# An attention stack on one core: phases written out, additions waited for one by one, values projected straight into the form in which they are used

## The chip, the core and the metric

One core of a Trainium2 chip. The kernel is one program; its time is the device time in microseconds (us) from start to end of the program. The engines are called as in the profile: PE (TensorE matmul), PEld (its weight load), DVE (VectorE), ACT (ScalarE), POOL (GpSimd) and SP (SyncE, which here only issues DMAs; SPq in the rows).

## The reference

The input is x, of 4 batches by 256 channels by 1024 positions, float32. Four attention layers follow one another. Layers 0 and 1 have one head each. Layers 2 and 3, which the change concerns, have eight heads of 32 channels:

```python
xn = group_norm(x) * gn_w + gn_b            # 32 groups
q, k, v = split(qkv_w @ xn + qkv_b)         # per head: 32 channels each
weight = softmax((q * s).T @ (k * s))       # 1024 x 1024 per head
a = weight @ v
hout = proj_w @ a + proj_b
return xn + hout                            # layer 2; layer 3 is x + hout in the same form
```

Each softmax row sums to one, so a constant added to every value (the value bias) comes through the attention unchanged.

## The kernel before

Layers 2 and 3 are done in one section (`eight_heads_in`). The work comes in 16 groups: 2 layers, 4 batches, 2 groups of 4 heads. A batch of a layer (two groups) is a round here. Each group has a phase of 64 steps. In one step PE makes one score tile (128 keys by 512 queries of one head, L1054), and ACT takes its exponential into a ring of four key tiles `PR` (L1226). A phase has two halves of the queries of 32 steps; in each half the eight key tiles (four heads each) pass through the ring. A key tile takes four steps.

For each key tile PE weighs the values (`weigh`, L957): four matmuls by 32 columns, one for each head, side by side in the array, into `psO`. In the profile a float32 matmul stands as two records, so a tile is 8 records and two tiles together 16. The sums of the exponentials are made in two ways. POOL adds key tiles 0 to 5 of a half in five additions into `PA` (L1268); the sum over keys of `PA` and of the last two tiles is made on PE by a matmul with ones (`sums`, L969, 24 records), which is the side unit "z". DVE then turns and inverts it and scales `psO` (`take_half`).

Beside the scores, PE does side units, each at a step of a table (`SIDE_AT`, `Z_AT`, `BN_AT`, `XN_AT`), in order, through four banks of `psD`:

- "m" and "a": 64 of them in a phase, score tiles of a later group (L1023), of which DVE takes the maxima (L1105). `EARLY` says how many of them stand in the phase before.
- "K", "Q": projections of the next group, 6 matmuls in each half (L89), taken by ACT into `SL` (L1191). ACT splits them into a high part `SH` (L1178), POOL makes the low part (`low`, L1251), and SP copies both by 24 DMAs into `KS` and `QS` (`stack`, L1298 and L1300). The next "K" must wait until these copies have landed (`stacks_filled`).
- "v", "w": in each phase the values of one group. "v" projects a half with channels on partitions (6 matmuls of 512 columns), ACT adds the bias into `VT`; "w" turns it round by four PE transposes (L1017), and ACT copies it into `V`.
- "p" in every second phase: the output projection of the round before (4 units). "t", "T": turned maxima.

In every second phase the next batch is normalised as well: POOL makes the factors, ACT writes the input at the steps of `XN_AT`, POOL makes its low part `XL` (L1245). Where layer 2 ends, POOL also splits the weights of layer 3 (L1277), which PE's next "K" waits for.

The waits around the change: before the first exponential of a key tile ACT waits for what is still read in its slot of the ring. At the first four tiles of a phase it waits for all five additions of the phase before:

```python
wait(e, av_done, weighed(P, J - 4))
if J >= 4: ...
else:
    wait(e, sum_done, ADDS * 2 * P)
```

In `sums` the two direct tiles come first and `PA` last; POOL's first addition of the next half waits for the whole unit. Phases 1 to 4 are two turns of a hardware loop (`Fori`), phases 9 to 14 three turns of another, the rest is written out. The last phase is followed by a tail: the sums and the output projection of the last half.

Of the kernel before, what the change touches and what calls it, by code (L numbers as in the profile page):

```python
# [5 lines left out]
ALU = mybir.AluOpType  # L6
# [32 lines left out]
def attention_stack(nc, x, w0, w1, w2, w3, wp1, wp2, wp3, par_d, ident_d, gmat_d, out):  # L39
    with ExitStack() as ctx:  # L40
# [90 lines left out]
        def single_heads():  # L131

            with ExitStack() as stage:
# [638 lines left out]
                def stack_copies(slot):  # L772
# [16 lines left out]
        EARLY = 10  # L789
# [47 lines left out]
        def taken(units, k, engine):  # L837

            return sum((u in "vwkqKQ") == (engine == "scalar") for u, _, _ in units[:k])
# [28 lines left out]
        WEIGH = [(0, 11), (1, 11), (2, 17), (3, 17), (4, 23), (5, 28), (6, 34), (7, 34)]  # L868
# [10 lines left out]
        def all_phases(e, phase):  # L879
# [22 lines left out]
        def eight_heads_in(stage):  # L902
# [4 lines left out]
            V = sb("V", [PART, GROUPS, NT, PART], F32, stage)  # L907
# [3 lines left out]
            WP = sb("WP", [PART, CT, C], F32, stage)  # L911
            VT = sb("VT", [PART, N], F32, stage)
# [16 lines left out]
            st_full, exp_done = sem("scores_full" + n), sem("exp_done" + n)  # L929
            av_done, sum_done, out_done = sem("av_done" + n), sem("sum_done" + n), sem("out_done" + n)  # L930
# [15 lines left out]
            with nc.Block() as block:  # L946
                @block.tensor
                def _(e):
                    def weigh(P, p, h, j):

                        if j == 0:
                            wait(e, out_done, 2 * P + h)
                        wait(e, exp_done, STEPS * P + QUADH * (NT * h + j + 1))
                        source = PR[:, j % 4, :].rearrange("p (q n) -> p q n", q=QUADH)
                        for q in range(QUADH):
                            cols = slice(CH * q, CH * q + CH)
                            mm = e.matmul(psO[cols, 0, :], V[:, p, j, cols], source[:, q, :], start=(j == 0), stop=(j == NT - 1))  # L957
# [3 lines left out]
                    def sums(full, P, h):  # L961

                        for j in (NT - 1, NT - 2, NT):
# [4 lines left out]
                            for q in range(QUADH):  # L968
                                mm = e.matmul(full[CH * q:CH * q + CH, :], ones[:, 0:CH], source[:, q, :],  # L969
                                              start=(j == NT - 1), stop=(j == NT))  # L970
                            if j == NT - 2:
# [3 lines left out]
                    def all_taken(place, r, k):  # L975

                        engine = "scalar" if k > 0 and UNITS[place][k - 1][0] in "vwkqKQ" else "vector"
# [9 lines left out]
                    def output(out_ap, i, group_halves, layer):  # L987
# [4 lines left out]
                        return split_products(e, out_ap, [(WP[:, t, o], A[:, t, mv]) for t in range(CT)])  # L992

                    def unit(place, r, k, P, p, G, g, norm, layers):
# [42 lines left out]
                    def phase(P, p, G, g, place, r, layers, proj=None, norm=None, norm_b=None):  # L1037
# [11 lines left out]
                        for s in range(STEPS):  # L1049
# [9 lines left out]
                            for j, at in WEIGH:  # L1059
                                if at + HALF_STEPS - STEPS == s and not (isinstance(P, int) and P == 0):  # L1060
                                    weigh(P - 1, 1 - p, 1, j)
                                for h in range(2):
                                    if at + HALF_STEPS * h == s:
                                        weigh(P, p, h, j)
# [15 lines left out]
                def _(e):  # L1080
# [18 lines left out]
                    def take(place, r, k, P, p, G, g, proj, norm, layers):  # L1099
# [3 lines left out]
                        if u in "am":  # L1103
# [7 lines left out]
                            top.then_inc(vec_free, 1)  # L1111
                        elif u == "z":
# [10 lines left out]
                    def phase(P, p, G, g, place, r, layers, proj=None, norm=None, norm_b=None):  # L1123
                        events = [(at, 0, k, "unit") for k, (u, at, i) in enumerate(UNITS[place])
                                  if u not in "vwkqKQ"]
# [24 lines left out]
                def _(e):  # L1150
                    def input_ready(place, r, G, norm, layers):
                        e.wait_ge(factors_done, norm + 1)
                        if place:
                            used = [x[::2] for x in UNITS[place]].index(("v", 1)) + 1
# [240 lines left out]
```

## Time and profile before

| | us |
|---|---|
| median of 3 runs (1725.8 to 1728.11) | 1725.93 |
| the profiled execution, its own time | 1731.05 |
| its span | 1729.3 |
| PE, POOL, DVE, ACT busy | 1595.8, 992.4, 1052.1, 898.7 |

The span is that of the instructions in the trace; the time has some 1.8 us more around it. Idle time stands in the rows as [us <- who ended it]. A matmul's duration is modelled and overlaps the next one, so on PE the distance from start to start counts.

### The profile page before, as it was taken

The numbers are of one execution on the slowest core, as the hardware profiler recorded it, in microseconds if no ns is written. First come the engines' busy times: TensorE is split into PE (matmuls) and PEld (weight loads), VectorE is DVE, ScalarE is ACT, GpSimd is POOL, SyncE is SP. The second block draws the span as 40 slices with busy tenths as digits, with TensorE's granted clock in tenths as the row PEclk, the third lists the DMA queues.
The fourth block names the chain that finished last, engine by engine and source line by source line (L and its number), as shares of the span: only waits on it lengthen the run. The fifth ranks groups of instructions, "written<-read, shape, count | busy, mean of one in ns | idle before, by whom it ended". The sixth has DMA issues, their size and how long they took to land.

```text
span 1729.3 us, 25134 instructions
## 1 busy us (share of the span) xinstructions
PE 1595.8 (92%) x8238; PEld 1007.0 (58%) x8238; DVE 1052.1 (61%) x1664; ACT 898.7 (52%) x1488; POOL 992.4 (57%) x394
## 2 busy tenths in 40 slices
PE   4888969999997789999999999999999999999996
PEld 2776758888886455554555555555555455555532
DVE  3566645454551566676776676677677667667641
ACT  3444414343433165656666656666565565655652
POOL 2222303121222168697698687878868779759875
PEclk7999989999999689999999999999999999999998
DMA  4000000000000501130230321303303123032000
GB/s 151 19 19 19 1 1 1 1 1 1 19 1 10 137 8 42 33 74 14 62 74 2 74 49 44 74 4 71 80 1 75 41 60 74 6 95 64 12 25 25
DMA packets 31481, 67.58 MB, mean 39 GB/s; under 512 B 7472, under 2 KB 9328, under 8 KB 31344
## 3 DMA queue, kind: packets, MB, share of 16 engines
q1 hardware_dynamic: 31344, 65.82, 15.5%
q8 instruction: 78, 1.28, 0.3%
q14 instruction: 59, 0.48, 0.1%
HBM read 7.82 MB, written 4.19 MB: 7 GB/s over the span
## 4 chain that ended last, share of the span: by engine, by line
PE 40%; POOL 13%; issue 5%; SPq 4%; ACT 2%; DVE 2%; DMA 1%; POOLq 1%; ACTq 0%; DVEq 0%
POOL PA L1268 11%; PE psD L89 9%; PE psD L1023 9%; PE psO L957 8%; PE psA L1054 7%; PE psD L969 5%; PE psO L1054 3%; SPq L1300 2%; SPq L1298 2%; POOL SL L1251 1%; ACT PR L1226 1%; DVE BNS L1105 1%; PE psD L1017 1%; DMA QS<-SL 1%; ACTq L1177 0%
## 5 line engine op out<-in xcount | busy, mean ns | idle before, releaser
L1105 DVE TENSOR_REDUCE BNS<-psD 128x1 f32<-128x512 f32 x1024 | 644.2, 683 | 267.4 <-PE psD L1023 266.4
L1268 POOL TENSOR_TENSOR PA<-PA,PR 128x2048 f32<-128x2048 f32 x128 | 586.8, 4584 | 40.1 <-ACT PR L1226 29.7
L1226 ACT ACTIVATE PR<-psA 128x512 f32<-128x512 f32 x688 | 394.3, 602 | 319.9 <-PE psA L1054 276.2
L1023 PE MATMUL psD<-KS,QS 96*128 96x512 f32 x1024 | 425.6, 421 | 22.7 <-ACT SL L1191 13.1
L1054 PE MATMUL psA<-QS,KS 97*128 97x512 f32 x688 | 302.7, 442 | 22.6 <-ACT PR L1226 12.0
L680 POOL TENSOR_SCALAR P<-P,RS 128x1024 f32<-128x1024 f32 x64 | 72.0, 1126 | 361.1 <-DVE RS L398 361.1
L957 PE MATMUL psO<-PR,V 128*32 128x512 f32 x2048 | 257.8, 610 | 2.2 <-DVE A L1090 2.0
L1226 ACT ACTIVATE PR<-psO 128x512 f32<-128x512 f32 x336 | 202.3, 602 | 104.2 <-PE psO L1054 77.8
L1023 PEld LDWEIGHTS psD<-KS,QS 96*128 96x128 f32 x1024 | 201.1, 197 | 76.1 <-ACT SL L1191 15.8
L1268 POOL TENSOR_TENSOR PA<-PR 128x2048 f32<-128x2048 f32 x32 | 147.1, 4598 | 167.7 <-PE psD L969 143.3
L1054 PEld LDWEIGHTS psA<-QS,KS 97*128 97x128 f32 x688 | 132.1, 193 | 180.2 <-ACT PR L1226 113.2
L1054 PE MATMUL psO<-QS,KS 97*128 97x512 f32 x336 | 142.7, 425 | 3.2 <-ACT PR L1226 3.1
L616 ACT ACTIVATE PTH<-psA 128x1024 fp32r<-128x1024 f32 x64 | 65.6, 1025 | 114.0 <-PE psA L283 114.0
L609 ACT ACTIVATE P<-psD,NM 128x1024 f32<-128x1024 f32 x64 | 71.2, 1113 | 96.4 <-DVE NM L391 96.4
L957 PEld LDWEIGHTS psO<-PR,V 128*32 128x32 f32 x2048 | 50.6, 110 | 119.2 <-issue 79.7
L391 DVE TENSOR_REDUCE NM<-psD 128x1 f32<-128x1024 f32 x64 | 77.6, 1214 | 61.3 <-PE psD L89 61.3
L298 PE MATMUL psO<-PTH,VH 128*128 128x512 f32 x256 | 106.5, 416 | 4.4 <-issue 3.2
L1251 POOL TENSOR_TENSOR SL<-SL,SH 128x1024 fp32r<-128x1024 f32 x34 | 80.2, 2378 | 45.6 <-ACT SH L1178 45.6
L1054 PEld LDWEIGHTS psO<-QS,KS 97*128 97x128 f32 x336 | 64.6, 192 | 70.4 <-ACT PR L1226 31.3
L298 PE MATMUL psO<-PTH,VL 128*128 128x512 f32 x256 | 102.4, 400 | 0.0
L298 PE MATMUL psO<-PTL,VH 128*128 128x512 f32 x256 | 102.2, 399 | 0.0
L404 DVE TENSOR_TENSOR PTL<-psA,PTH 128x1024 fp32r<-128x1024 f32 x64 | 78.2, 1222 | 37.8 <-ACT PTH L616 37.6
(148 smaller groups left out, 2017.1 us busy)
## 6 DMA issues: line engine op xcount, KB each, us to landing
KS<-SH SPq DMA_DIRECT2D x128, 128.0 KB, 2.3
QS<-SH SPq DMA_DIRECT2D x128, 128.0 KB, 2.4
KS<-SL SPq DMA_DIRECT2D x64, 128.0 KB, 2.4
QS<-SL SPq DMA_DIRECT2D x64, 128.0 KB, 2.4
X<-x SPq DMA_DIRECT2D x4, 1024.0 KB, 7.3
out<-X SPq DMA_DIRECT2D x4, 1024.0 KB, 4.3
XN<-w SPq DMA_DIRECT2D x2, 768.0 KB, 7.7
KH<-KL SPq DMA_DIRECT2D x8, 128.0 KB, 2.3
```

What stands on the lines that cost most here:

```text
L89: last = e.matmul(out_ap, w, m, start=(i == 0), stop=(i == len(terms) - 1))
L298: mm = e.matmul(psO[:, t, :], vv[:, s, cols], pp[:, h, s, :], start=(s == k == 0), stop=(s == NT - 1 and k == 2))
L391: e.tensor_reduce(NM[:, g % 4:g % 4 + 1], psD[:, index[u] % 2, :], AX.X, ALU.max, negate=True).then_inc(max_done, 1)
L404: e.tensor_tensor(PTL[:, i // 4, :, cols], psT.rearrange("p (s t) -> p s t", s=NT), PTH[:, i // 4, :, cols].bitcast(F32), ALU.subtract).th ...
L957: mm = e.matmul(psO[cols, 0, :], V[:, p, j, cols], source[:, q, :], start=(j == 0), stop=(j == NT - 1))
L969: mm = e.matmul(full[CH * q:CH * q + CH, :], ones[:, 0:CH], source[:, q, :], start=(j == NT - 1), stop=(j == NT))
L1023: mm = e.matmul(full, QS[0:STACK, group, int(u == "a"), q, tile * PART:(tile + 1) * PART], KS[0:STACK, group, q, h * HALF:(h + 1) * HALF], ...
L1054: e.matmul(score_bank(s, p), KS[0:STACK + 1, p, q, j * PART:(j + 1) * PART], QS[0:STACK + 1, p, h, q, :], start=True, stop=True).then_inc( ...
L1105: top = e.tensor_reduce(MXH[:, h, q, tile:tile + 1], full, AX.X, ALU.max)
L1226: e.activation(PR[:, J % 4, (s % QUADH) * HALF:(s % QUADH + 1) * HALF], score_bank(s, p), ACT.Exp, scale=scale).then_inc(exp_done, 1)
L1251: e.tensor_tensor(SL[:, which, :].bitcast(F32R), SL[:, which, :], SH[:, which, :], ALU.subtract).then_inc(low_done, 1)
L1268: e.tensor_tensor(PA[:, :], PR[:, (J - 1) % 4, :] if j == 1 else PA[:, :], PR[:, J % 4, :], ALU.add).then_inc(sum_done, 1)
```

## The change

- The two `Fori` loops become Python loops: all phases are written out.
- "w" and `VT` are gone. "v" now makes the values of both groups of a batch at once with keys on partitions: four units per batch, each 12 matmuls of 256 columns, all in the second phase of a round (g = 1), copied by ACT into one `V` of [128, 8, 256] (before, one `V` for each group). PE's weighing of that phase waits for each copy.
- The value bias goes into the output bias once: a unit "b" before the first phase, 16 records of one column, added by DVE. Both output weights are loaded at the start (`WP[2]`, `WP[3]`) instead of one after the other.
- ACT waits for four instead of five additions before the first tile of a phase, and before tile 3 of each half for the unit "z". `sums` begins with `PA`, which has its own semaphore `sums_read` for POOL, and tile 6 is released before tile 7.
- The tables: weighing goes in four pairs in a half instead of three pairs and two singles; "z" two steps earlier; "K" of the first phase of a round from 15.5 and 31 to 23 and 25, of the second from 41 and 44 to 47 and 49; "p" and the normalisation are moved too.

```diff
-        EARLY = 10
+        EARLY = 12
-        XN_AT = (32, 34, 36, 36)
-        BN_AT = (8.5, 10.5, 12.5, 14.5)
-        SIDE_AT = [{"v": (9, 13), "w": (21.5, 26), "K": (15.5, 31), "Q": (39.5, 41)},
-                   {"v": (8.5, 15), "w": (20, 27), "K": (41, 44), "Q": (46, 53), "p": (12.5, 28.5, 36, 56)}]
-        Z_AT = (39, 8)
-        FIRST_AT = {"k": (0.1, 0.2), "q": (0.3, 0.4), "v": (1, 1.1), "w": (2, 2.1), "K": (8, 10), "Q": (12, 14)}
+        XN_AT = (31, 34, 35, 36)
+        BN_AT = (7.5, 10.5, 15.5, 16.5)
+        SIDE_AT = [{"K": (23, 25), "Q": (37.5, 39.5)},
+                   {"v": (6.8, 7.4, 21, 22.5), "K": (47, 49), "Q": (55, 57.5), "p": (15, 39, 16, 23.5)}]
+        Z_AT = (37, 6)
+        FIRST_AT = {"k": (0.1, 0.2), "q": (0.3, 0.4), "b": (1,), "K": (8, 10), "Q": (12, 14)}
...
-        WEIGH = [(0, 11), (1, 11), (2, 17), (3, 17), (4, 23), (5, 28), (6, 34), (7, 34)]
+        WEIGH = [(0, 10), (1, 10), (2, 19), (3, 19), (4, 28), (5, 28), (6, 33), (7, 33)]
...
-            with e.Fori(0, B - 2) as r:
+            for r in range(B - 2):
...
-            with e.Fori(B, ROUNDS - 1) as r:
+            for r in range(B, ROUNDS - 1):
...
+                        if place is not None and p == h == j % 2 == 0:
+                            value = [k for k, (u, _, i) in enumerate(UNITS[place]) if (u, i) == ("v", j // 2)][0]
+                            e.wait_ge(act_free, base_of("scalar", place, r) + taken(UNITS[place], value + 1, "scalar"))
...
-                        for j in (NT - 1, NT - 2, NT):
+                        for j in (NT, *range(NT - DIRECT, NT)):
...
+                            if j == NT:
+                                mm.then_inc(sums_read, 1)
+                            elif j < NT - 1:
                                 mm.then_inc(av_done, 1)
...
                         elif u == "v":
-                            mm = project(full, 2 * C + PART * g, i)
-                        elif u == "w":
-                            halves_v = [j for j, (name, _, _) in enumerate(UNITS[place]) if name == "v"]
-                            all_taken(place, r, halves_v[i] + 1)
-                            for n in range(NT // 2):
-                                st = slice(i * HALF + n * PART, i * HALF + (n + 1) * PART)
-                                mm = e.transpose(full[:, n * PART:(n + 1) * PART], VT[:, st], ident[:, :])
+                            for j in range(2):
+                                st = slice((2 * i + j) * PART, (2 * i + j + 1) * PART)
+                                mm = split_products(e, full[:, j * C:(j + 1) * C],
+                                                    [(xx[:, t, st], w[:, t, 2 * C:3 * C])
+                                                     for xx, w in ((XH, WH), (XL, WH), (XH, WL)) for t in range(CT)])
...
-                                wait(e, av_done, weighed(P, J - 4))
+                                if J % NT == 3:
+                                    if J >= NT or not (isinstance(P, int) and P == 0):
+                                        sums_of = [x[::2] for x in UNITS[place]].index(("z", 1 - J // NT))
+                                        e.wait_ge(d_full, base_of("all", place, r) + sums_of + 1)
+                                else:
+                                    wait(e, av_done, weighed(P, J - 4))
...
-                                    wait(e, sum_done, ADDS * 2 * P)
+                                    wait(e, sum_done, ADDS * 2 * P - max(ADDS - 4 - J, 0))
...
-                                    before = [k for k, (u, _, i) in enumerate(UNITS[place]) if u == "z" and i == 1 - h][0]
-                                    e.wait_ge(d_full, base_of("all", place, r) + before + 1)
+                                    e.wait_ge(sums_read, 2 * P + h)
```

## Rows read from the trace of the kernel before

**Rows 1.** The page: PE's busy time, and the granted clock in 40 slices.
```profile
PE 1595.8 (92%) x8238; PEld 1007.0 (58%) x8238; DVE 1052.1 (61%) x1664; ACT 898.7 (52%) x1488; POOL 992.4 (57%) x394
PEclk7999989999999689999999999999999999999998
```
**Rows 2.** Windows of rounds, phases 1 to 14: length, busy PE PEld DVE ACT POOL, clock.
```profile
674.70:815.80 141.10, 134.94 (x722) 74.39 (x720) 97.33 (x165) 86.27 (x154) 112.42 (x39) 0.99 0.20 46
...
951.40:1093.90 142.50, 136.22 (x722) 75.41 (x720) 96.33 (x164) 86.75 (x154) 111.49 (x38) 0.98 0.21 51
1093.90:1228.70 134.80, 133.19 (x721) 73.47 (x720) 95.86 (x164) 85.31 (x153) 107.80 (x36) 1.00 0.22 50
1228.70:1370.80 142.10, 136.55 (x722) 74.85 (x720) 97.57 (x166) 86.19 (x154) 111.16 (x39) 0.98 0.20 46
...
1509.30:1646.50 137.20, 136.07 (x720) 74.53 (x721) 94.94 (x162) 84.81 (x151) 105.61 (x36) 0.98 0.24 62
```
**Rows 3.** Timeline of PE around a pair of weighed tiles and around a single one.
```profile
1423.64 0.39 PE L1023 MATMUL psD<-KS,QS 96*128 96x512 f32 x1
1423.96 1.92 PE L957 MATMUL psO<-PR,V 128*32 128x512 f32 x16
...
1426.15 0.40 PE L1023 MATMUL psD<-KS,QS 96*128 96x512 f32 x1
...
1428.50 0.39 PE L1023 MATMUL psD<-KS,QS 96*128 96x512 f32 x1
1428.82 1.06 PE L957 MATMUL psO<-PR,V 128*32 128x512 f32 x8
...
1430.15 0.40 PE L1023 MATMUL psD<-KS,QS 96*128 96x512 f32 x1
```
**Rows 4.** The chain that ended last, PE's side units: start, us, what.
```profile
1390.33 1.38 PE psD L89 x6
...
1396.57 0.44 PE psD L1017 x4
...
1411.60 2.71 PE psD L969 x24
```
**Rows 5.** Timeline of PE in layer 1, whose value units have 256 columns.
```profile
356.77 0.40 PE L89 MATMUL psD<-WH,XL 128*128 128x256 f32 x2
357.01 0.40 PE L89 MATMUL psD<-WL,XH 128*128 128x256 f32 x2
```
**Rows 6.** Timeline at the start of phase 2.
```profile
746.18 0.50 PE L1054 MATMUL psA<-QS,KS 97*128 97x512 f32 x1 [1.05 <-ACT PR L1226]
```
**Rows 7.** Waits from 674.7 to 1646.5: total us, times, longest.
```profile
ACT PR L1226 <- POOL PA L1268: 25.5, 8, 3.6
```
**Rows 8.** Timeline at the turn of the first loop, end of phase 2.
```profile
815.80 0.55 PE L1054 MATMUL psA<-QS,KS 97*128 97x512 f32 x1 [2.51 <-issue]
```
**Rows 9.** Window behind that turn: same columns as rows 2.
```profile
816.10:819.50 3.40, 3.40 (x14) 1.72 (x16) 2.08 (x3) 1.79 (x3) 1.50 (x1) 0.50 0.21 46
```
**Rows 10.** Timeline around the start of phase 5: POOL's low parts, ACT's "K".
```profile
951.19 4.74 POOL L1251 TENSOR_TENSOR SL<-SL,SH 128x1024 fp32r<-128x1024 f32 x2
...
974.79 0.69 ACT L1191 ACTIVATE SL<-psD,PAR 128x512 f32<-128x512 f32 x1 [3.23 <-DMA QS<-SL]
```
**Rows 11.** Timeline of PE in phase 6, first "K" of layer 3.
```profile
1068.10 0.70 PE L89 MATMUL psD<-XH,WH 128*128 128x512 f32 x2 [3.13 <-POOL WL L1277]
```
**Rows 12.** Page, costliest groups: POOL's additions.
```profile
L1268 POOL TENSOR_TENSOR PA<-PA,PR 128x2048 f32<-128x2048 f32 x128 | 586.8, 4584 | 40.1 <-ACT PR L1226 29.7
```
**Rows 13.** Timeline ahead of the first phase: ACT takes the first half of values.
```profile
553.87 0.69 ACT L1191 ACTIVATE VT<-psD,PAR 128x512 f32<-128x512 f32 x1 [0.67 <-PE psD L89]
```
**Rows 14.** Timeline of DVE in phase 15: `take_half`, first and last operation.
```profile
1686.23 0.72 DVE L1084 STREAM_TRANSPOSE sums_turned<-psD 128x512 f32<-128x512 f32 x1 [16.48 <-PE psD L969]
...
1688.15 0.69 DVE L1090 TENSOR_TENSOR A<-psO,A 128x512 f32<-128x512 f32 x1
```
**Rows 15.** Timeline of PE in the tail: the last sums.
```profile
1709.71 1.33 PE L969 MATMUL psD<-PA,ones 128*32 128x512 f32 x8 [2.71 <-POOL PA L1268]
```

More of the change, by code:

```diff
@@ L837, in taken @@
         def taken(units, k, engine):
-            return sum((u in "vwkqKQ") == (engine == "scalar") for u, _, _ in units[:k])
+            return sum((u in "vkqKQ") == (engine == "scalar") for u, _, _ in units[:k])
         UNITS = [side_units(0, True), side_units(1, True), side_units(0), side_units(1), side_units(0, last=True)]
@@ L956, in weigh @@
                             cols = slice(CH * q, CH * q + CH)
-                            mm = e.matmul(psO[cols, 0, :], V[:, p, j, cols], source[:, q, :], start=(j == 0), stop=(j == NT - 1))
+                            mm = e.matmul(psO[cols, 0, :], V[:, j, PART * p + CH * q:PART * p + CH * q + CH], source[:, q, :], start=(j == 0), stop=(j == NT - 1))
                         if j < NT - DIRECT:
@@ L975, in all_taken @@
                     def all_taken(place, r, k):
-                        engine = "scalar" if k > 0 and UNITS[place][k - 1][0] in "vwkqKQ" else "vector"
+                        engine = "scalar" if k > 0 and UNITS[place][k - 1][0] in "vkqKQ" else "vector"
                         count = min(k, 0) + taken(UNITS[place], max(k, 0), engine)
@@ L991, in output @@
                         e.wait_ge(wp_loaded[layer], 16)
-                        return split_products(e, out_ap, [(WP[:, t, o], A[:, t, mv]) for t in range(CT)])
+                        return split_products(e, out_ap, [(WP[layer][:, t, o], A[:, t, mv]) for t in range(CT)])
                     def unit(place, r, k, P, p, G, g, norm, layers):
@@ L1063, in phase @@
                                     if at + HALF_STEPS * h == s:
-                                        weigh(P, p, h, j)
+                                        weigh(P, p, h, j, place, r)
                     def tail():
@@ L1111, in take @@
                             top.then_inc(vec_free, 1)
+                        elif u == "b":
+                            for layer in (2, 3):
+                                bias = e.tensor_tensor(par(f"bp{layer}", 2), par(f"bp{layer}", 2), full[:, CT * layer:CT * layer + CT], ALU.add)
+                            bias.then_inc(vec_free, 1)
                         elif u == "z":
@@ L1153, in input_ready @@
                         if place:
-                            used = [x[::2] for x in UNITS[place]].index(("v", 1)) + 1
+                            used = [x[::2] for x in UNITS[place]].index(("v", NT // 2 - 1)) + 1
                             e.wait_ge(d_full, base_of("all", place, r) + used)
@@ L1157, in input_ready, with run @@
                                 stacks_filled(e, G)
-                    def run(what, k, place, r, G, g, norm, norm_b, layers):
+                    def run(what, k, place, r, P, G, g, norm, norm_b, layers):
                         if what == "x":
@@ L1181, in run @@
                         e.wait_ge(d_full, base_of("all", place, r) + k + 1)
-                        if u == "w":
-                            wait(e, av_done, (G - 1) * 2 * PIECES)
-                            e.activation(V[:, g, i * NT // 2:(i + 1) * NT // 2, :].rearrange("p t c -> p (t c)"), full,
-                                         ACT.Copy).then_inc(act_free, 1)
+                        if u == "v":
+                            wait(e, av_done, 2 * PIECES * P - (1 if i < NT // 2 - 1 else 0))
+                            e.activation(V[:, 2 * i:2 * i + 2, :].rearrange("p t c -> p (t c)"), full, ACT.Copy).then_inc(act_free, 1)
                         else:
@@ L1188, in run @@
                                 stacks_filled(e, G)
-                            bias = (par(f"bv{layers[0]}", 2)[:, g:g + 1] if u == "v"
-                                    else par(f"bqk{layers[1]}", 4)[:, 2 * gg + which:2 * gg + which + 1])
-                            e.activation(VT[:, mv] if u == "v" else SL[:, which, mv], full, ACT.Identity,
-                                         bias=bias).then_inc(act_free, 1)
+                            bias = par(f"bqk{layers[1]}", 4)[:, 2 * gg + which:2 * gg + which + 1]
+                            e.activation(SL[:, which, mv], full, ACT.Identity, bias=bias).then_inc(act_free, 1)
                     def phase(P, p, G, g, place, r, layers, proj=None, norm=None, norm_b=None):
@@ L1211, in phase @@
                             for x in events:
-                                run(*x[2:], place, r, G, g, norm, norm_b, layers)
+                                run(*x[2:], place, r, P, G, g, norm, norm_b, layers)
                             return
@@ L1228, in phase @@
                             while events and events[0][0] <= s:
-                                run(*events.pop(0)[2:], place, r, G, g, norm, norm_b, layers)
+                                run(*events.pop(0)[2:], place, r, P, G, g, norm, norm_b, layers)
                     all_phases(e, phase)
```

28 lines of the change are left out of this document (16 added, 12 removed).

## The prediction

> **What bounds the kernel now.** I read the page first: PE is busy 92% of the span, nobody else over 61% [rows 1]. A busy PE is modelled, so the next question is whether its instructions stand close together. The timeline says they do: a score and a maxima tile take 0.47 us together, 0.235 us each from start to start, for hundreds of them, and where a group of another kind stands between them the next one follows at once [rows 3]. I then cut the trace into rounds of 128 steps [rows 2]. They do the same work (720 to 722 matmul records) but take 134.8 to 142.5 us. So each round is a sum of PE's work, about 133 us, plus stalls, and the stalls can be read off one by one. The best round, phases 7 and 8, is my base (of seven, five stand in the rows); the seven rounds run from 674.7 to 1646.5, 971.8 us, which is 28.2 us over seven times 134.8. Layers 0 and 1 are untouched.
>
> By the Trainium skill ("Trainium Kernel Development and Optimization", "Reading a trace") weight-load time, not matmul time, tells how near the roofline a kernel is. Weight loads are 54% of a round here [rows 2]; the spacing of the matmuls contradicts it as a bound, and I keep it as a rival.
>
> **The change part by part.**
>
> *Values.* Before, a round has four "v" of 1.38 us and four "w" of 0.44 us [rows 4], 7.3 us of PE. After, it has four units of 12 matmuls of 256 columns. Layer 1 has this form in its value units: two matmuls in 0.24 us [rows 5]. That is 48 x 0.12 = 5.76 us. PE saves 1.5 us a round, 10.6 us over seven. ACT saves about half of its eight copies, which is off the path. The single `V` makes copies urgent: the first must be there at step 10, having been projected at 6.8; PE does about 2.5 us of work in between, ACT needs 0.6 us for each copy, so I cost the wait at nothing; if it is not covered it is the slower rival below.
>
> *Weighing in pairs.* From L1023 to L1023 a pair takes 1426.15 - 1423.64 = 2.51 us, less 0.47 for the score and maxima tile: 2.04. A single takes 1.65 - 0.47 = 1.18 [rows 3]. Two singles become one pair in each half: 2.36 - 2.04 = 0.32 us, 28 halves, 9.0 us. The rows show a step of 0.32 us into a group and 0.33 us out of it where 0.235 is usual. The Trainium skill ("TensorEngine Tiling (Array Packing)", "Key Properties") says a change of tiling mode drains the engine; by that rule fewer groups are cheaper, and the trace agrees with about 0.2 us a group.
>
> *Start of a phase.* In seven or eight phases ACT waits up to 3.6 us for POOL's fifth addition [rows 7]; PE then stands 1.05 us [rows 6]. The first tile only needs the fourth addition, which ends 4.6 us earlier [rows 12], and "z" two steps earlier with `PA` first lets POOL begin sooner. I take 1.1 us a round away, 7.7 us.
>
> *Loops.* At each of three turns PE stands 2.5 us, released by nothing but issue [rows 8], and then runs 3.4 us at the 1.2 GHz level, half of 2.4 [rows 9], which costs 1.7 us more. Phases 5 to 8 are already written out and show no such gap, so I cost written-out code at nothing.
> The Trainium skill ("Runtime: NRT & Kernel Launch", "Instruction fetch mechanics") says that a taken branch breaks the sequential prefetch of instructions while straight code streams. By that rule all three gaps go and none comes; the trace agrees in both.
>
> *"K" and the DMAs.* In phases 1, 5 and 9 ACT can't take "K" at step 17 until 24 DMAs have landed; the low parts end at 955.9 and the last lands at 974.8, 18.9 us later [rows 10]. PE loses 1.8 to 2.7 us, and again time at half clock. The new "K" stands at 23, taken at step 24. Counting steps of the shorter phase: 25 x 0.47 + 3 pairs 6.1 + "z" 2.9 + one "K" 1.4 + 1.0 for a turned row and a small wait = 23.1 us. Low parts should end about 4.5 us into the phase, the DMAs at 23.3. So the wait shrinks to 0.3 us at most phases. After phase 0 and phase 6, where POOL is later (6 and 7 us), some 1.5 and 3 us stay, clock included.
>
> *Layer 3's weights.* PE waited 3.13 us [rows 11] at step 41, plus half clock. "K" at 47 comes six steps, over 3.3 us, later: gone.
>
> Loops, "K" and weights together are what lifts rounds over the base: 28.2 us removed, and of what the base itself has, 0.4 us of "K" wait a round, 2.8 us.
>
> *What is added.* In the first phase of a round nothing but four score and maxima pairs, 1.9 us, stands between "z" at 6 and the weighing at 10, which needs DVE's scaled half, 2.6 us from its first operation to the end of its last [rows 14]; 0.6 us a round, 4 us. "K" leftovers 7 x 0.3 + 1.5 + 3 = 6.6 us. In the tail the 16 direct records now come behind the last addition instead of in its shadow. PE's last eight take 1.33 us there [rows 15]; the other 16 cost 1.7 us at full clock, by the 2.71 us of 24 records [rows 4], and 3.5 at half, on the path; 2 us. Ahead of the first phase ACT's copy of "v" stands before the split of "K" and "Q": it waits 0.67 and takes 0.69 us [rows 13], and all behind it (POOL, 24 DMAs) comes 1.4 us earlier. The second output weight is one more DMA issue of 0.6 us, long before anything waits; "b" runs while PE waits for the stacks. The moves of "p", `XN_AT` and `BN_AT` keep their order and I cost them at nothing: POOL's factors should come at 36.5 us of the phase, ACT reaches step 31 at about 37.9.
>
> Sum: -10.6 - 9.0 - 7.7 - 28.2 - 2.8 + 4 + 6.6 + 2 - 1.4 = -47.1 us. Against the profiled 1731.05 that is 1684; the median of the runs is 5.1 us below the profiled execution, so 1679 us.
>
> **Is somebody else the bound then?** A round falls to about 131 us. POOL has 20 additions of 4.58 us in it, 91.7 us [rows 12], and 106 to 112 us in all [rows 2], a chain with waits. I followed it: in the shorter phase (59 us) the second half's additions can only begin after tile 9, at 40.6 us, and end at 64.4, which is 5.5 us into the next phase, where "z" at step 6 stands at 5.3 us. So that chain has almost no slack at one place in each round: 0.2 us is lost by my count, but every late us there is one of PE's.
>
> **The rivals.**
> 1. *POOL becomes the bound.* For it: the slack of nothing just worked out, and POOL's additions that follow back to back. Against it: the other half of the round has 2 us or more to spare. If POOL's chain is 2 to 4 us longer at that point in a round, and PE then loses clock too, the gain falls by 14 to 30 us: 1693 to 1709.
> 2. *PE's matmuls aren't the bound* (the weight-load rule): the 19.6 us of saved PE work bring nothing, the stalls go: 1679 + 20 = 1699. For it: only 54% of weight load; against it: rounds differ by their stalls alone.
> 3. *The single `V` stalls PE, slower than before.* ACT's copy must come between "v" at 6.8 and 7.4 and step 10, behind an exponential that itself waits for "z". A missed copy stops PE, as "K" did in phase 5: about 2 us and 1.7 us of lost clock, 3.7 us. The gain of 47 us is eaten by 13 such stops, two in each of seven rounds; with three (78 us) the time is 1757. Against it: POOL, not ACT, has been the late one in all rows, and ACT is busy only 63% of a round.
> 4. *Written-out code stalls on its instructions.* Ten more phases of straight code; if they paid what a turn pays once each, 10 x 4.2 = 42 us, the time would be 1721. Against it: phases 5 to 8.
>
> **How the numbers follow.** The forecast, 1679, has 0.76; its own range is 1667 to 1692: lower where all leftovers and added waits (12 us) vanish, higher by a half more of each. Rival 1 has 0.13, rival 2 0.04, rival 3 0.04, rival 4 0.03. The range that leaves two in ten out is 1665 to 1700. A measurement of this kernel tells 0.2% (3.5 us) from no change. Faster 0.95, within 0.2% 0.02 (rival 4, or a mild form of 3), slower 0.03.
>
> **What the profile after would show.** Round windows of about 131 us with PE over 97% busy, the first phase of a round about 59 us and the second 72; no gap of 2.5 us ended by issue, and the clock at 1.0 in almost all rounds. PE records of 256 columns at 0.12 us spacing in a unit of 12; no L1017. ACT waiting for POOL's `PA` under 1 us. "K" of the first phase waits under 1 us except in phases 1 and 7. At the end 24 sum records behind POOL's last addition. I am wrong if rounds stand over 134 us, which would mean a new chain through POOL or the copies, seen as PE idle ended by ACT or POOL at step 1 to 10, or if "z" waits for the fifth addition over 1 us in every round.

## The result and the profile after

The changed kernel takes 1679.29 us (median of 4 runs, 1676.54 to 1680.55) against 1725.87 us before (4 runs, 1720.66 to 1728.11). The ratio is 0.9736, with a 95% interval of 0.9718 to 0.9754: 46.6 us or 2.6% faster. Forecast were 1679 us and 47.1 us less.

The near match flatters the working. The sum was made against the profiled execution of before, and between the two profiled executions the span fell by 54.5 us (1729.3 to 1674.8). That of before lay 5.1 us above its median, that of after 2.8 below. So the sum of 47.1 us was 7 us short of what it was made for, as the table below shows by stage; that the medians agree with it to 0.5 us is luck.

Windows of the kernel after, one for each round, with the columns of [rows 2], then the last phase with the tail, then phase 0:

```profile
674.20:805.20 131.00, 129.82 (x729) 74.33 (x728) 95.52 (x164) 82.59 (x149) 108.90 (x37) 1.00 0.21 49
805.20:935.90 130.70, 129.80 (x729) 74.36 (x728) 95.52 (x164) 82.59 (x149) 108.02 (x37) 1.00 0.22 49
...
1067.00:1200.40 133.40, 130.09 (x729) 74.28 (x729) 95.56 (x165) 82.59 (x149) 111.56 (x37) 1.00 0.21 48
1200.40:1331.10 130.70, 129.78 (x729) 74.28 (x728) 95.52 (x164) 82.53 (x149) 108.13 (x37) 1.00 0.21 49
...
1461.90:1593.00 131.10, 129.87 (x730) 74.37 (x729) 95.56 (x164) 82.59 (x150) 108.15 (x37) 1.00 0.26 65
1593.00:1674.80 81.80, 66.49 (x318) 25.19 (x316) 23.86 (x40) 33.31 (x66) 50.84 (x13) 0.91 0.03 13
605.70:674.20 68.50, 64.06 (x343) 39.64 (x344) 45.13 (x78) 44.26 (x78) 51.47 (x22) 0.95 0.00 1
```

Rounds that took 134.8 to 142.5 us [rows 2] now take 130.7 to 131.1, one of them 133.4. PE is busy for 99% of a round and its clock stays at full rate, where before some rounds had 0.98. The stages side by side:

| stage | before | after | change | forecast |
|---|---|---|---|---|
| start to phase 0 | 607.5 | 605.7 | -1.8 | -1.4 |
| phase 0 | 67.2 | 68.5 | +1.3 | 0 |
| phases 1 to 14 | 971.9 | 918.8 | -53.1 | -47.7 |
| last phase and tail | 82.7 | 81.8 | -0.9 | +2 |

The first phase of a round is 59.1 to 59.5 us long (61.8 in phase 7), the second 71.6 to 71.9; the forecast was 59 and 72.

Only the row of phases 1 to 14 stands clear of what single executions differ by. In the other three rows the differences are as large as that spread: in the eleven variants of the changed kernel below, the stretch up to phase 0 takes 603.0 to 606.9 us, and phase 0 takes 65.7 to 67.8 us. The last phase with its tail takes 82.7 us here before the change, and 79.0 in the one other execution of that code (experiment 1); after the change it takes 81.8, and 82.0 to 85.7 in five variants that keep its additions and its order of the sums (experiments 2, 3, 4, 5 and 8).

Three places of PE's timeline after: a part of a value unit in phase 8, the pair that waits for DVE in the first phase of a round, and "K" in phase 7:

```profile
1137.84 0.40 PE L89 MATMUL psD<-WH,XH 128*128 128x256 f32 x2
1138.08 0.40 PE L89 MATMUL psD<-WH,XL 128*128 128x256 f32 x2
...
815.10 0.39 PE L1033 MATMUL psD<-KS,QS 96*128 96x512 f32 x1
816.15 1.92 PE L960 MATMUL psO<-PR,V 128*32 128x512 f32 x16 [0.66 <-DVE A L1100]
...
1094.87 0.50 PE L1033 MATMUL psD<-KS,QS 96*128 96x512 f32 x1 [2.43 <-ACT SL L1203]
```

Two value matmuls take 0.24 us from start to start, as forecast, and a whole unit of 12 takes 1.43 us. From 815.10 to 816.15 are 1.05 us where 0.32 is usual [rows 3]: 0.73 us lost, in six first phases, and 1.1 us in phase 13. I had said 0.6. In phase 7 the copies are late, as I had said, by 2.4 us for PE. Waits of phases 1 to 14 after:

```profile
ACT PR L1242 <- POOL PA L1283: 14.3, 15, 1.9
PE psO L960 <- DVE A L1100: 5.0, 7, 1.0
ACT SL L1203 <- DMA QS<-SL: 4.4, 3, 3.3
```

ACT still waits for additions, 15 times: in each second phase 0.6 to 0.9 us for the fourth addition and 1.0 to 1.3 us for the fifth, and once 1.9 us. The forecast had said under 1 us. PE has no stop behind it. The last sums, as PE's timeline shows them after, the counterpart of [rows 15]:

```profile
1653.73 1.94 PE L972 MATMUL psD<-PA,ones 128*32 128x512 f32 x8 [3.85 <-POOL PA L1283]
1655.41 2.77 PE L972 MATMUL psD<-PR,ones 128*32 128x512 f32 x16
```

The 16 direct records stand behind POOL's last addition. They once ran in its shadow.

### The profile page after: what moved, and what is told of

It reads as the page before. It is cut to its first block, busy times and chain, and to the rows that moved or that the text cites. A ratio compares the mean times of both kernels' runs of the same rounds, so it can differ in the third digit from the quotient of the medians.

```text
span 1674.8 us, 22024 instructions
## 1 busy us (share of the span) xinstructions
PE 1558.9 (93%) x8318; PEld 1008.5 (60%) x8318; DVE 1048.1 (63%) x1666; ACT 875.8 (52%) x1456; POOL 991.7 (59%) x394
## 4 chain that ended last, share of the span: by engine, by line
PE 54%; POOL 6%; DVE 3%; SPq 2%; ACT 1%; issue 1%; POOLq 0%; DMA 0%; DVEq 0%; ACTq 0%
PE psO L960 12%; PE psD L1033 12%; PE psD L89 11%; PE psA L1064 9%; PE psD L972 5%; POOL PA L1283 5%; PE psO L1064 5%; DVE BNS L1115 2%; ACT PR L1242 1%; SPq L1316 1%; SPq L1314 1%; POOL SL L1267 1%; DVE sums_turned L1094 0%; DVE A L1098 0%; DVE A L1100 0%
## 5 line engine op out<-in xcount | busy, mean ns | idle before, releaser
L1033 PE MATMUL psD<-KS,QS 96*128 96x512 f32 x1024 | 417.7, 413 | 22.4 <-DMA QS<-SL 10.7
L1064 PE MATMUL psA<-QS,KS 97*128 97x512 f32 x688 | 291.1, 425 | 3.3 <-DMA QS<-MROW 1.6
L960 PE MATMUL psO<-PR,V 128*32 128x512 f32 x2048 | 249.5, 604 | 8.2 <-DVE A L1100 6.3
L1064 PEld LDWEIGHTS psA<-QS,KS 97*128 97x128 f32 x688 | 130.8, 190 | 111.8 <-issue 57.4
L1064 PE MATMUL psO<-QS,KS 97*128 97x512 f32 x336 | 146.9, 437 | 0.7 <-ACT PR L1242 0.7
L960 PEld LDWEIGHTS psO<-PR,V 128*32 128x32 f32 x2048 | 53.6, 110 | 131.4 <-issue 82.7
L616 ACT ACTIVATE PTH<-psA 128x1024 fp32r<-128x1024 f32 x64 | 65.6, 1024 | 110.9 <-PE psA L283 110.9
L1064 PEld LDWEIGHTS psO<-QS,KS 97*128 97x128 f32 x336 | 63.7, 190 | 83.5 <-issue 45.6
```

The source lines that it names most:

```text
L960: mm = e.matmul(psO[cols, 0, :], V[:, j, PART * p + CH * q:PART * p + CH * q + CH], source[:, q, :], start=(j == 0), stop=(j == NT - 1))
L1033: mm = e.matmul(full, QS[0:STACK, group, int(u == "a"), q, tile * PART:(tile + 1) * PART], KS[0:STACK, group, q, h * HALF:(h + 1) * HALF], ...
L1064: e.matmul(score_bank(s, p), KS[0:STACK + 1, p, q, j * PART:(j + 1) * PART], QS[0:STACK + 1, p, h, q, :], start=True, stop=True).then_inc( ...
```

## The experiments

Where a start of a phase is given, it is that of its first score tile, the 64 x n + 1st of L1064 (L1054 before). All ratios are to the kernel before on the same chip. Differences to the changed kernel are between medians; where the ratios give another size, it stands beside. In the windows of two phases that are shown, phases 4 and 5, the second phase of one round and the first of the next stand together; such a window is as long as a round.

**1. Only the loops written out.**

```diff
-            with e.Fori(0, B - 2) as r:
+            for r in range(B - 2):
...
-            with e.Fori(B, ROUNDS - 1) as r:
+            for r in range(B, ROUNDS - 1):
```

> The kernel before with only the two loops written out. By my account three turns of 2.5 us and 1.7 us of lost clock go, 12.6 us: 1713. But phases 3, 11 and 13, which follow a turn, are the ones whose 'K' showed no wait for the DMAs: the gap had given the copies time. If so, that wait comes back there, about 3.5 us with its lost clock each, and only 2 us are gained: 1724. The trace tells the two apart by ACT's waits for 'K' in phases 3, 11 and 13. Rival 4 (written-out code stalls on its instructions): slower than 1726.

Measured 1717.98 us, ratio 0.9942 (0.9922 to 0.9961), 9 us faster: between the two accounts. The three gaps at the turns are gone, and ACT now waits for the copies in phases 3, 11 and 13 too, as the expectation had it, though less (3.1, 3.1 and 1.8 us). PE stops behind it in phases 3 and 11. ACT and PE in phase 3 of this kernel:

```profile
840.79 0.69 ACT L1191 ACTIVATE SL<-psD,PAR 128x512 f32<-128x512 f32 x1 [3.05 <-DMA QS<-SL]
...
841.53 0.50 PE L1023 MATMUL psD<-KS,QS 96*128 96x512 f32 x1 [1.44 <-ACT SL L1191]
```

The waits for these copies rise from 4 with 12.9 us (phases 1, 5, 7 and 9) to 6 with 18.4 (phases 1, 3, 7, 9, 11 and 13). So a gap at a turn had covered a part of a wait, and not all of the 12.6 us came in. That phase 5 lost its wait, with no turn right ahead of it, shows that the place where the copies come late moves for other reasons too, which were not followed.

**2. The changed kernel with its loops rolled up.** The same edit in the other direction.

> The changed kernel with both loops rolled up again. 'K' now stands where the copies have landed, so nothing hides behind the gap: three turns at 4.2 us, 12.6 us slower, 1692. If the turn only costs what the rest of the change didn't already cover, less than 5 us.

Measured 1682.61 us, ratio 0.9742 (0.9725 to 0.9758). It can't be told from the changed kernel's 0.9736. The first turn shows a gap:

```profile
802.96 0.40 PE L1033 MATMUL psD<-KS,QS 96*128 96x512 f32 x1
804.86 0.50 PE L1064 MATMUL psA<-QS,KS 97*128 97x512 f32 x1 [1.51 <-issue]
```

The other two turns show none: phases 10 and 12 are 71.5 us long, like phase 8. Before, the three had 2.5, 2.5 and 2.3 us. Against the changed kernel, phase 2 is 1.2 us longer and phases 11 and 13, which follow a turn, are 0.4 and 0.3 us longer: some 2 us for three turns, not 12.6. Phase 7, which is in no loop, is 3.4 us longer, with 6.8 us at the 1.2 GHz level; experiment 5, without loops, has the same, so this is not the turns. My account of this term was wrong: a turn has no fixed price.

**3. "K" early again.**

```diff
-        SIDE_AT = [{"K": (23, 25), "Q": (37.5, 39.5)},
+        SIDE_AT = [{"K": (15.5, 31), "Q": (37.5, 39.5)},
```

> The changed kernel with 'K' of the first phase of a round back at steps 15.5 and 31. Step 17 is now reached 17.5 us into the phase, the copies land at 23.3: ACT waits over 5 us, PE some 4.8 us and 1.7 to 3.4 us of clock behind it, in each of seven phases: 35 to 50 us slower, 1714 to 1729. That would be all that the change brings. If the place of 'K' hardly matters, under 10 us.

Measured 1736.15 us, ratio 1.0073 (1.0044 to 1.0102): slower than the kernel before, 57 us slower than the changed one, more than the 35 to 50 expected. ACT's waits in two phases, in its timeline:

```profile
698.08 0.69 ACT L1203 ACTIVATE SL<-psD,PAR 128x512 f32<-128x512 f32 x1 [6.71 <-DMA QS<-SL]
837.03 0.69 ACT L1203 ACTIVATE SL<-psD,PAR 128x512 f32<-128x512 f32 x1 [5.63 <-DMA QS<-SL]
```

The window of phases 4 and 5:

```profile
880.70:1019.60 138.90, 132.94 (x728) 75.48 (x728) 95.73 (x164) 83.16 (x149) 107.72 (x37) 0.98 0.20 46
```

The first phase of a round takes 67.3 to 69.6 us instead of 59.2. PE stands idle for 5.1 to 8.6 us each time, where 4.8 was expected, and in phases 1 to 14 it runs 55 us at the 1.2 GHz level, none in the changed kernel.

**4. One more group in each half.**

```diff
-        WEIGH = [..., (4, 28), (5, 28), ...]
+        WEIGH = [..., (4, 23), (5, 28), ...]
```

> The changed kernel with tile 4 weighed at step 23 instead of with tile 5 at 28, so one more group in each half. If PE's matmuls are the bound: 0.32 us in each of 28 halves, 9 us slower, 1688. If weight loads are the measure, nothing: the same number of loads and matmuls, 1679.

Measured 1691.38 us, ratio 0.9794 (0.9777 to 0.981), 12 us slower than the changed kernel (10 by the ratios). A first phase is 60.3 us (59.2), a second 72.4 (71.6): 1.9 us a round, 0.5 us a half instead of 0.32. Laid beside the changed kernel step by step, the extra group itself costs 0.3 us in each half, as forecast. The rest comes once in a phase, around its second half or its end: 0.4 us in a first phase, 0.3 us in a second; what makes it was not found. Weight loads and matmuls are the same in number, so the load time alone does not set the pace.

**5. Less work in the value units.** The product of XH with the low part of the weights is left out.

```diff
-                                                     for xx, w in ((XH, WH), (XL, WH), (XH, WL)) for t in range(CT)])
+                                                     for xx, w in ((XH, WH), (XL, WH)) for t in range(CT)])
```

> The changed kernel without the third product (XH by WL) in the value units; the values lose their low weight part. 16 matmuls of 256 columns less in a round, 1.92 us by 0.12 us each. If PE is the bound: 13.4 us faster over seven rounds, 1666. If POOL is the bound (rival 1) or weight loads aren't touched enough: under 4 us, 1676 or more.

Measured 1671.17 us, ratio 0.9672 (0.9655 to 0.9688), 8 us faster than the changed kernel (11 by the ratios), where 13.4 was expected. A second phase falls from 71.6 to 70.4: 1.2 us of the 1.92 us of work taken out. So PE's work counts there, but not in full. Laid beside the changed kernel step by step, phase 10 has gained 0.9 us behind the first two value units and loses 0.3 of it between steps 9 and 10, where a maxima tile waits for DVE. It has gained 1.6 us behind all four and loses 0.4 of it at steps 33 to 38. There ACT waits for the normalisation factors of POOL, which come only some 0.7 us sooner. ACT's wait in phase 10, first in the changed kernel, then here:

```profile
ACT PR L1242 <- POOL SC L129: 0.4, 1, 0.4
ACT PR L1242 <- POOL SC L129: 1.3, 1, 1.3
```

Together that is the other 0.7 us. In this profiled execution, the slowest of the four, phase 7 and the last phase with its tail are also 3.5 and 3.9 us longer than in that of the changed kernel, with PE at the 1.2 GHz level for longer.

**6. The sums in the old order.** The direct tiles first, then `PA`; POOL waits for the whole unit. Of the two direct tiles, tile 6 stays ahead of tile 7, as in the changed kernel; before the change it was the other way round.

```diff
-                        for j in (NT, *range(NT - DIRECT, NT)):
+                        for j in (*range(NT - DIRECT, NT), NT):
...
-                            if j == NT:
-                                mm.then_inc(sums_read, 1)
-                            elif j < NT - 1:
+                            if j < NT - 1:
...
-                                    e.wait_ge(sums_read, 2 * P + h)
+                                    before = [k for k, (u, _, i) in enumerate(UNITS[place]) if u == "z" and i == 1 - h][0]
+                                    e.wait_ge(d_full, base_of("all", place, r) + before + 1)
```

> The changed kernel with the sums in the old order: the two direct tiles first, PA last, POOL waiting for the whole unit. By my account POOL's first addition waits for tile 9's exponential, not for the sums, so the rounds don't change, and the tail gets its 16 records back into the shadow of the last addition: 2 us faster, 1677. If POOL is the bound (rival 1): POOL starts up to 1.8 us later in each half, 10 to 25 us slower.

Measured 1667.76 us, ratio 0.9688 (0.9659 to 0.9717), about 8 us faster than the changed kernel by the ratios, 12 by the medians, where 2 was expected. The last phase and tail take 77.8 us instead of 81.8, and a second phase 71.4 instead of 71.6 to 71.9. The last sums:

```profile
1641.87 1.90 PE L972 MATMUL psD<-PR,ones 128*32 128x512 f32 x16
1645.93 1.06 PE L972 MATMUL psD<-PA,ones 128*32 128x512 f32 x8 [2.17 <-POOL PA L1282]
```

The new order of the sums is a part of the change that costs, and the early release of POOL brings nothing in the rounds. How much the order costs is less sure. Of the 10 us between the two profiled executions 2.7 lie ahead of phase 0, where the programs are the same. Of the 4.0 us in the last phase 3.2 are there by step 52, as two falls of the clock which the changed kernel has by then, of 3.4 us each, are missing here up to 47 us into the phase; no run shows what ties them to the order.

**7. POOL adds half of the columns.** All additions but those of the first half of phase 0 leave out columns 1024 to 2047.

```diff
+                                half = slice(0, QUADH * HALF if P is None or (isinstance(P, int) and P == 0 and h == 0) else QUADH * HALF // 2)
-                                e.tensor_tensor(PA[:, :], PR[:, (J - 1) % 4, :] if j == 1 else PA[:, :],
-                                                PR[:, J % 4, :], ALU.add).then_inc(sum_done, 1)
+                                e.tensor_tensor(PA[:, half], PR[:, (J - 1) % 4, half] if j == 1 else PA[:, half],
+                                                PR[:, J % 4, half], ALU.add).then_inc(sum_done, 1)
```

> The changed kernel with POOL adding only half of the columns, so half of the sums are wrong; an addition takes some 2.3 us. If PE is the bound, rounds stay within 0.5 us, and only the last phase with its tail (POOL's chain, 10 x 2.3 us less where ACT and PE allow), phase 0 and phase 7 gain: 12 to 20 us, 1660 to 1667. If POOL is the bound (rival 1), rounds fall by several us each and the time below 1650.

Measured 1661.96 us, ratio 0.9647 (0.9617 to 0.9678), 17 us faster (15 by the ratios), as expected if PE is the bound. The window of phases 4 and 5:

```profile
863.80:994.40 130.60, 129.83 (x728) 74.28 (x729) 95.57 (x164) 82.54 (x149) 64.20 (x37) 1.00 0.22 49
```

POOL's busy time falls from 108 to 64 us and the round stays at 130.6. POOL is not the bound of a round. Phase 7 falls to 59.2 (from 61.8), and the last phase with its tail to 70.8 (from 81.8).

**8. ACT waits for all five additions again.**

```diff
-                                    wait(e, sum_done, ADDS * 2 * P - max(ADDS - 4 - J, 0))
+                                    wait(e, sum_done, ADDS * 2 * P)
```

> The changed kernel with ACT waiting again for all five additions before the first tile of a phase. After the first phase of a round the fifth ends by my count 5.5 us into the next phase, so ACT stands some 5 us and PE, which has a pair to weigh and two steps in hand, 2.5 us, in seven phases: 18 us slower, 1697. If the two earlier steps of 'z' alone had removed the wait, no difference.

Measured 1714.12 us, ratio 0.993 (0.9903 to 0.9958): 35 us slower than the changed kernel (33 by the ratios), for one number in one wait; 18 was expected. The timeline of ACT and PE at the start of phase 2:

```profile
737.63 1.08 ACT L1242 ACTIVATE PR<-psA 128x512 f32<-128x512 f32 x2 [5.52 <-POOL PA L1283]
738.28 0.50 PE L1064 MATMUL psA<-QS,KS 97*128 97x512 f32 x1 [2.81 <-ACT PR L1242]
```

The window of phases 4 and 5:

```profile
867.00:1003.50 136.50, 133.16 (x729) 75.34 (x729) 96.00 (x164) 82.98 (x149) 107.95 (x37) 0.97 0.21 47
```

ACT waits 5.5 us and PE stands 2.8 (2.5 in most rounds), as worked out. The second phase is 76.1 to 77.3 us long instead of 71.6 to 71.9, 4.2 to 5.7 us more. The rest of it is the clock: PE runs 3.4 us at the 1.2 GHz level behind the stop in phase 2, 6.8 us behind each of the other six, 44 us in all, and half of it is lost. Phase 2, with the longer stop and the shorter stretch at the low level, is the one with 4.2 us. I had left the clock out.

**9. The last phase's additions on VectorE.** DVE gets them as events behind each key tile; the edit is the `add` of experiment 12, for both halves, and the sums stay in the new order.

> The changed kernel with the ten additions of the last phase on VectorE instead of POOL. VectorE has only 20 maxima there. I estimate 2.3 us for an addition, from 1.2 us for 1024 columns in the transposes' low part. Then POOL's chain of 23 us in each half gives way to ACT's and PE's 17 to 25 us: last phase and tail 10 to 14 us shorter, 1665 to 1669. If the chain isn't what ends the kernel, no difference.

Measured 1672.84 us, ratio 0.9708 (0.9682 to 0.9735). The last phase and tail take 77.7 us instead of 81.8, less than half of the 10 to 14 us expected. An addition takes 2.28 us on DVE, 4.6 on POOL, but in the first half it stands in front of maxima, for which PE then waited 0.7 and 2.1 us.

**10. Additions on VectorE, first pair at 11, "K" at 25 and 27.**

```diff
-        SIDE_AT = [{"K": (23, 25), "Q": (37.5, 39.5)},
+        SIDE_AT = [{"K": (25, 27), "Q": (37.5, 39.5)},
...
-        WEIGH = [(0, 10), (1, 10), ...]
+        WEIGH = [(0, 11), (1, 11), ...]
```

> As the one with additions on VectorE, and the first pair weighed at step 11 instead of 10 and 'K' at 25 and 27 instead of 23 and 25. Step 11 takes the 0.7 us of wait for the scaled half out of each first phase (5 us over seven), 'K' two steps later takes 1 us off the wait in phase 7: 6 us faster than that kernel, 1660. If the later 'K' and pair shift the wait elsewhere (ring slot of tile 0, 'Q'), no gain.

Measured 1684.82 us, ratio 0.9767 (0.9743 to 0.9791): slower by 12 us than experiment 9, so the expectation failed. First phases take 61.1 us, second 72.1. The wait for DVE's scaled half is gone and another took its place, as the waits of this kernel say:

```profile
PEld psD L1033 <- DVE BNS L1115: 19.4, 48, 1.8
PE psD L1033 <- DVE BNS L1115: 7.5, 7, 1.4
```

The first of these stops in PE's timeline, in phase 1:

```profile
683.64 0.49 PE L1033 MATMUL psD<-KS,QS 96*128 96x512 f32 x1 [1.03 <-DVE BNS L1115]
```

With the pair one step later, a fifth maxima tile stands between "z" and the pair. Four have gone through the four banks while DVE scales, and the fifth must wait for DVE. The two edits can be told apart by place, in phases 8 and 9 beside those of the changed kernel. The later pair costs a first phase 1.2 us, half of it in each half, and a second phase 0.5. The other 0.8 us of a first phase come at step 33, behind the moved "K", and phase 8, whose "K" was not moved, has nothing there.

**11. The changed code with the old tables.**

```diff
+        EARLY = 10
+        XN_AT = (32, 34, 36, 36)
+        BN_AT = (8.5, 10.5, 12.5, 14.5)
+        SIDE_AT = [{"K": (15.5, 31), "Q": (39.5, 41)},
+                   {"v": (8.5, 9.2, 17.5, 20), "K": (41, 44), "Q": (46, 53), "p": (12.5, 28.5, 36, 56)}]
+        Z_AT = (39, 8)
+        WEIGH = [(0, 11), (1, 11), (2, 17), (3, 17), (4, 23), (5, 28), (6, 34), (7, 34)]
```

> The changed code with the old tables (EARLY, XN_AT, BN_AT, 'K', 'Q', 'p', 'z', weighing), values at 8.5, 9.2, 17.5 and 20. Written out, with the new values and waits, but 'K' at 15.5 and singles: 9 us for the singles and 25 to 40 us for 'K' in front of its copies, as phases are now shorter: 1713 to 1728, so that the code alone brings almost nothing. If the code brings the gain and the tables are details: under 1695.

Measured 1724.03 us, ratio 0.9993 (0.998 to 1.0006): no gain that can be measured. ACT's waits for the copies:

```profile
ACT SL L1203 <- DMA QS<-SL: 31.8, 7, 5.8
```

They were 12.9 us in 4 waits before. The work saved on PE brought the phase to "K" sooner, and it waited there.

**12. The two faster variants together.** The edit of experiment 6, and the five additions of the last half on VectorE:

```diff
+                    def add(P, J):
+                        h, j = J // NT, J % NT
+                        wait(e, exp_done, STEPS * P + QUADH * (J + 1))
+                        if j == 1:
+                            e.wait_ge(d_full, base_of("all", 4, None) + [x[::2] for x in UNITS[4]].index(("z", 0)) + 1)
+                        wait(e, sum_done, ADDS * (2 * P + h) + j - 1)
+                        e.tensor_tensor(PA[:, :], PR[:, (J - 1) % 4, :] if j == 1 else PA[:, :],
+                                        PR[:, J % 4, :], ALU.add).then_inc(sum_done, 1)
...
+                        if place == 4:
+                            events += [(QUADH * (NT + j + 1), 1, NT + j, "add") for j in range(1, ADDS + 1)]
...
+                            if what == "add":
+                                add(P, k)
...
-                        for h in range(2):
+                        for h in range(2 if place < 4 else 1):
```

> The two variants that were faster, together: the sums in the old order, and in the last phase the five additions of the second half on VectorE, 2.28 us each instead of 4.6. The last addition then ends at the last exponentials instead of behind them. With the old order alone, PE's last matmuls with PA waited 2.2 us for POOL and the last phase with its tail took 77.8 us; VectorE should take 3 to 4 us off: 1664. If the old order has already taken all that the tail had to give, 1668.

Measured 1664.59 us (median of 5), ratio 0.9643 (0.961 to 0.9677): 3.6% faster than before, the fastest kernel that computes everything. The window of the last phase and tail:

```profile
1587.20:1658.60 71.40, 60.13 (x318) 23.56 (x316) 35.27 (x45) 33.47 (x66) 28.24 (x8) 1.00 0.04 15
```

DVE's last addition, in its timeline:

```profile
1634.39 2.29 DVE L1141 TENSOR_TENSOR PA<-PA,PR 128x2048 f32<-128x2048 f32 x1 [0.40 <-ACT PR L1253]
```

71.4 us instead of 81.8, and 6.4 us less than the 77.8 of experiment 6, where 3 to 4 were expected. The clock is at 1.00 in this stretch instead of 0.91 in the changed kernel and 0.92 in experiment 6, so a part of the gain is clock. The addition now waits for ACT, not ACT and PE for it. By its interval it overlaps with experiment 6; the stage shows the difference in one execution of each: up to step 60 of the last phase the two run alike to 0.1 us, and behind it this one is ahead.

## Why the prediction was right, point by point

- **PE's work plus stalls makes the round.** Right. I expected 131 us for a round and 59 and 72 for its phases; they are 130.7 to 131.1, 59.2 and 71.6. These came from the count step by step; the terms of the sum add up to 132.0 a round, and 131.3 is what the seven take on average. Experiment 7 shows that POOL isn't the bound (rival 1), experiment 4 that the time moves with the weight loads unchanged (rival 2). Experiment 5 limits it: 0.7 of 1.92 us of work taken out of a second phase came back as waits for DVE and for POOL's factors.
- **Values.** Right, by the trace. The forecast size was 1.5 us a round. From start to start "v" and "w" took 7.1 us of PE in a round, and the four value units take 5.7: 1.4 us. No variant takes this term back by itself. `V` never stalled PE: no wait of PE for ACT's value copies stands among the waits after, so rival 3 didn't occur.
- **Weighing in pairs.** Right. Experiment 4 finds the 0.3 us in each half where the extra group stands. It cost 10 to 12 us in all and not 9, as a phase then loses another 0.3 to 0.4 us elsewhere.
- **Start of a phase.** Right in kind, mis-sized. I priced it at the 1.1 us that stood there before. Without the new wait the shortened phase would stall ACT for 5.5 us and lose 4.2 to 5.7 us, clock included, in each round (experiment 8). The near-zero slack that I had found was this place. Letting POOL begin sooner by the new order of the sums brings nothing (experiment 6).
- **Loops.** The step that fails. Three turns at 4.2 us were counted as 12.6 us of the 28.2. Alone they gave 9 us, as a part came back as waits for "K" (experiment 1), and in the changed schedule some 2 us by stage, which the medians can't tell from nothing (experiment 2). That written-out code costs nothing holds (rival 4 is out): the kernel of experiment 1 has no stop of that kind. The rule of the Trainium skill on taken branches ("Runtime: NRT & Kernel Launch", "Instruction fetch mechanics"), which I had found in agreement, does not say what a turn costs here: two of three turns in experiment 2 show no gap.
- **"K" and the DMAs.** Right that the wait had to go, and in phase 7 the leftover came (2.4 us of PE, and a phase 2.6 us longer than the others). In phase 1 the 1.5 us did not come, nor the 0.3 us in each of the seven. This is most of what the sum was short by in phases 1 to 14: 6.6 us of leftovers were forecast, 2.6 came. But the term was valued by what stood there before, 1.8 to 2.7 us in three phases. Left at its old step "K" costs 57 us (experiment 3), as all seven first phases then wait.
- **Layer 3's weights.** Right. Phase 6 fell from 76.5 to 71.9 us, the stop is gone; with the old tables it is 76.4 (experiment 11).
- **What is added.** The wait for the scaled half was 0.73 us for 0.6. POOL's factors were forecast ahead of ACT, at 36.5 us of the second phase; ACT waits 0.4 us for them in each, until 38.3. In the tail the 16 records came behind the last addition, as said. Whether they cost the 2 us can't be told from the one row of the table: it shows 0.9 us less, but the last phase before takes 82.7 us in one execution and 79.0 in another, with the clock at 0.91 and 0.94, so what looks like a gain is no more than this spread. The 1.3 us more of phase 0 is of the same kind; in the variants it takes 65.7 to 67.8.

The terms are not additive. Code without tables gives nothing (experiment 11); the tables' "K" taken back loses all (experiment 3); one wait taken back loses three quarters (experiment 8). The account by stage worked because it added up the phase as it would be, step by step, and looked for what is late in it, not because each removed stall was worth its old length.

Open is why the turn of a loop shows 2.3 to 2.5 us before and mostly nothing after, and where the clock falls in the last phase.

## What to carry to other kernels

When work is taken out of a stage with a written order, lay out the shorter stage step by step and ask of each wait when its releaser comes; here the work saved brought nothing (0.9993) until "K" was moved behind its copies and one addition less was waited for. Value a stall by what it would be in the new stage, with the clock that a stop of PE costs behind it. Look at the tail by itself: five additions moved to an idle engine and the direct sums put back into a shadow took 10 us off the last 82, clock included, by one execution of each.

## What the hardware showed that I had not expected

- A turn of a hardware loop left PE idle for 2.3 to 2.5 us at all three turns of one schedule [rows 8] and, in another schedule of the same loop, 1.5 us at one turn and nothing at two.
- Stops of PE of 2.5 to 2.8 us at the start of a phase lengthened it by 4.2 to 5.7 us; in all, 44 us of phases 1 to 14 then ran at the 1.2 GHz level, none in the changed kernel, which has no such stop there. Its seven stops of 0.7 to 1.1 us left the clock at full rate, and so did one of 2.4 us in phase 7, where one of 2.3 us in experiment 9 was followed by 3.4 us at the low level.
- An addition of 128x2048 float32 took 2.28 us on VectorE and 4.59 us on GpSimd.
